# Two three-pass MLPs with rounded halves become one program of sixteen groups with plain fp32 products

## What is computed

```python
    xt = x_text + y                      # y: convolution result, scaled and shifted
    h = layernorm(xt, g_ffn, b_ffn)
    h = gelu(h @ W1 + b1) @ W2 + b2      # 512 -> 2048 -> 512
    xt = xt + h
    return layernorm(xt, g_norm_out, b_norm_out)
x = _layernorm(x + xattn(x, ...))
# second MLP; the linear maps around its gelu are folded into w3, b3, w4 earlier in the kernel
x = _layernorm(x + (gelu(x @ w3 + b3) @ w4 + b_con + down_bias))
```

## Time and profile before

| what | value |
|---|---|
| median of three runs | 5240.5 us |
| profiled execution, its time | 5239.47 us |
| profiled execution, first to last instruction (span) | 5237.8 us |
| span of the two MLP stages, from the barrier ahead of m1 | 3601.8 to 5237.8 us |
| TensorE matmul busy, of the span | 4067.8 us (78%) |
| mean granted TensorE clock | 0.88 of full speed |

### The profile page before, as it was taken

One profiled execution on the slowest core, in us unless ns is written; L12 is line 12 of the kernel. 1 busy time (PEld: TensorE's weight loads), 2 busy tenths in 40 slices (PEclk: granted clock), 3 DMA queues, 4 the chain that ended last, 5 costly groups with the idle time before them and its releaser, 6 DMA issues. The chain is left out here.

```text
span 5237.8 us, 64936 instructions
## 1 busy us (share of the span) xinstructions
PE 4067.8 (78%) x20932; PEld 3324.4 (63%) x20932; DVE 2781.6 (53%) x9228; ACT 1439.7 (27%) x2178; POOL 1430.1 (27%) x1238
## 2 busy tenths in 40 slices
PE   2243599975787784867769959696999996799998
PEld 2241277763676774756748847575788885688887
DVE  8965334443898998998815545423243433222222
ACT  1125423323555553545510010122111110211111
POOL 2530000000212111112106603202576763233332
PEclk9556799987888887888889979897999998899999
DMA  0003412225010010010014322334121211200000
GB/s 11 18 20 101 125 55 79 81 66 183 27 43 29 10 40 27 18 33 29 7 68 143 136 93 108 126 111 136 58 77 60 72 62 46 69 23 26 18 28 18
DMA packets 236653, 325.12 MB, mean 62 GB/s; under 512 B 67154, under 2 KB 117202, under 8 KB 234066
## 3 DMA queue, kind: packets, MB, share of 16 engines
q1 hardware_dynamic: 144260, 170.98, 11.0%
q10 hardware_dynamic: 89568, 142.64, 8.0%
q0 software_dynamic: 2560, 8.39, 0.4%
HBM read 214.93 MB, written 107.00 MB: 61 GB/s over the span
## 5 line engine op out<-in xcount | busy, mean ns | idle before, releaser
L1459 PE MATMUL xa_ps_t<-xa_diag,xa_s_buf 128*128 128x128 f32 x4096 | 501.1, 283 | 166.8 <-DVE xa_s_buf L1640 99.1
L2785 DVE CAST m_act_hl<-m_g 128x512 fp32r<-128x512 f32 x256 | 138.0, 539 | 891.8 <-ACT m_g L2673 891.8
L1459 PEld LDWEIGHTS xa_ps_t<-xa_diag,xa_s_buf 128*128 128x128 f32 x4096 | 485.2, 197 | 196.8 <-DVE xa_s_buf L1640 116.2
L1588 DVE MAX8 xa_cand<-xa_s_buf 128x8 f32<-128x64 f32 x4096 | 535.0, 217 | 119.2 <-issue 56.9
L2534 POOL TENSOR_TENSOR m_act_hl<-m_g,m_act_hl 128x512 fp32r<-128x512 f32 x256 | 352.5, 1377 | 701.2 <-DVE m_act_hl L2785 701.2
L2673 ACT ACTIVATE m_g<-m_ps_h,m_b 128x512 f32<-128x512 f32 x256 | 176.5, 690 | 1103.9 <-PE m_ps_h L82 1103.9
L1404 POOL TENSOR_TENSOR xa_aT<-xa_a,xa_aT 128x512 fp32r<-128x512 f32 x128 | 159.8, 1270 | 1004.1 <-ACT xa_a L1524 1004.1
L80 PE MATMUL m_ps_h<-m_hT,m_w 128*128 128x512 f32 x1024 | 412.8, 403 | 12.3 <-DVE m_w L2764 7.6
L81 PE MATMUL m_ps_h<-m_hT,m_w 128*128 128x512 f32 x1024 | 405.0, 395 | 0.0
L82 PE MATMUL m_ps_h<-m_hT,m_w 128*128 128x512 f32 x1024 | 404.8, 395 | 0.0
L82 PE MATMUL m_ps_o<-m_w,m_act_hl 128*128 128x512 f32 x1024 | 404.4, 395 | 0.0
(11 more groups left out here) (371 smaller groups left out, 8411.5 us busy)
## 6 DMA issues: line engine op xcount, KB each, us to landing
at_xk<-in_x_dram SPq DMA_DIRECT2D x128, 128.0 KB, 2.7
spectrum<-df_yo ACTq DMA_DIRECT2D x32, 512.0 KB, 2.8
id_raw<-spectrum SPq DMA_DIRECT2D x32, 512.0 KB, 3.8
m_xt<-x ACTq DMA_DIRECT2D x64, 256.0 KB, 3.6
ky_raw<-in_ctx_dram SPq DMA_DIRECT2D x16, 768.0 KB, 6.4
xa_ks<-kt SPq DMA_DIRECT2D x48, 256.0 KB
xa_raw<-in_ctx_dram SPq DMA_DIRECT2D x32, 384.0 KB, 3.5
w<-bf_out_t SPq DMA_DIRECT2D x32, 256.0 KB, 2.4
```

Source lines behind the costliest of these rows:

```text
L1459: last = pe.matmul(ps_t[:, c // 4, c % 4, :], s_buf[:, t % 2, h, k0:k0 + P], diag[:, h, :], start=(h == 0 and c % 4 == 0), stop=(h == HEAD ...
L1588: dve.max(out=ranks[h][:, :, g], in_=s_buf[:, t % 2, h, g * SEG:(g + 1) * SEG])
```

## The change

One `stage_mlps` takes the place of the two calls. It has 16 groups, of which `mlp(g)` = 0 for the first eight and 1 for the rest, all written out in order without a loop. `mm3` is replaced by one `pe.matmul` on fp32 tiles; w1 and w2 have both MLPs' weights side by side where the two halves were. The halves' instructions are gone on all engines. The weights come by DMA straight into place: W1 and W2 in four slabs each at the start, w3 and w4 in one DMA of 4 MB each, issued while groups 2 and 3 run. g_ffn and b_ffn are now applied where ScalarE writes hT (`written`, four activations of 128x128 a tile). The three operations of `outer_sum`, on GpSimd before, are on VectorE (`outer`) for every tile. All loads and stores go through SyncE's queue in one order. The second MLP turns tiles straight from xt, which has three group slots. turn comes at chunks 4, 7, 10 and 13.

```diff
-        w1 = sb("w1", [P, 2, DC, HID], F32R)
-        w2 = sb("w2", [P, 2, HC, D], F32R)
...
-        xt = sb("xt", [P, 2, Q, D])
-        h = sb("h", [P, D])
-        hT = sb("hT", [P, 2, 2, DC, N], F32R)
-        act_hl = sb("act_hl", [P, 2, 2, N], F32R)
-        g32 = sb("g32", [P, N])
+        w1 = sb("w1", [P, 2, DC, HID])
+        w2 = sb("w2", [P, 2, HC, D])
...
+        xt = sb("xt", [P, 3, Q, D])
+        fac = sb("fac", [P, 2, 3, D])
+        h = sb("h", [P, 2, D])
+        hT = sb("hT", [P, 2, DC, N])
+        gelu = sb("gelu", [P, 2, N])
...
+                def load(g, q):
+                    i = Q * g + q
+                    if g >= 3:
+                        sp.wait_ge(s_n1, i - 3 * Q + 1)
+                    if mlp(g) == 0:
+                        if i >= 2:
+                            sp.wait_ge(s_mod, i - 1)
+                        for n, v in enumerate((conv, so_in, sh_in)):
+                            sp.dma_start(fac[:, q % 2, n, :], rows(v, i * P, P)).then_inc(s_in[q % 2], 16)
+                        src = rows(x1, i * P, P)
                     else:
-                        n = m - PIECES // 2
...
-                    sp.dma_start(xt[:, 1, m % Q, :], src).then_inc(s_raw[m % Q], 16)
+                        j = i - Q * HALF
+                        sp.wait_ge(s_tr, i - 1)
+                        sp.wait_ge(s_st[q % 2], 16 * (j // 2 + 1))
+                        src = rows(x2, j * P, P)
+                    sp.dma_start(xt[:, g % 3, q, :], src).then_inc(s_in[q % 2], 16)
...
+                load(0, 0)
+                load(0, 1)
+                up_slab(0)
+                load(0, 2)
+                down_slab(0)
+                load(0, 3)
+                for s in range(1, SLABS):
+                    up_slab(s)
+                    down_slab(s)
+                load(1, 0)
+                load(1, 1)
...
+                    outer = g >= 1 and mlp(g - 1) == 0
+                    if outer:
+                        again(g - 1, 0)
+                    if g + 1 < GROUPS:
+                        load(g + 1, 2)
+                    if outer:
...
+                    if g == 2:
+                        sp.dma_start(w1[:, 1, :, :], w3.rearrange("(c p) n -> p c n", p=P)).then_inc(s_v1, 16)
+                    if g == 3:
+                        sp.dma_start(w2[:, 1, :, :], w4.rearrange("(c p) n -> p c n", p=P)).then_inc(s_v2, 16)
...
+                for g in range(GROUPS):
+                    nxt = mlp(g + 1) if g + 1 < GROUPS else None
+                    if nxt == 0:
+                        modulate(g + 1, 0)
+                    for q in range(Q):
+                        if g >= 1:
+                            power("e", Q * (g - 1) + q)
+                        if nxt == 0:
+                            power("p", Q * (g + 1) + q)
+                            if q + 1 < Q:
+                                modulate(g + 1, q + 1)
+                        if g >= 1 and mlp(g - 1) == 0:
+                            power("f", Q * (g - 1) + q)
+                        if nxt is not None:
+                            bias(g + 1, q)
...
                     for c in range(DC):
-                        w_hi, w_lo = (w1[:, x, c, n * P:(n + 1) * P] for x in range(2))
-                        last = mm3(pe, ps_h[:, n % 2, :], w_hi, w_lo, hT[:, slot, 0, c, :], hT[:, slot, 1, c, :],
-                                   start=(c == 0), stop=(c == DC - 1))
+                        last = pe.matmul(ps_h[:, n % 2, :], w1[:, mlp(g), c, n * P:(n + 1) * P], hT[:, g % 2, c, :],
+                                         start=(c == 0), stop=(c == DC - 1))
...
-                        a_hi, a_lo = (act_hl[:, n % 2, x, q * P:(q + 1) * P] for x in range(2))
-                        last = mm3(pe, ps_o[:, q, :], a_hi, a_lo, w2[:, 0, n, :], w2[:, 1, n, :],
-                                   start=(n == 0), stop=(n == HC - 1))
+                        last = pe.matmul(ps_o[:, q, :], gelu[:, n % 2, q * P:(q + 1) * P], w2[:, mlp(g), n, :],
+                                         start=(n == 0), stop=(n == HC - 1))
...
-                if modulated:
-                    pe.wait_ge(s_c, 16 * 6)
-                    for m in range(PIECES // 2):
...
-                        pe.wait_ge(s_raw[m % Q], 16 * (m // Q + 1))
-                        for r in range(4):
-                            n = 4 * q + r
-                            last = pe.matmul(ps_o[:, 0, c * HC + n:c * HC + n + 1], xt[:, 1, m % Q, r * P:(r + 1) * P],
-                                             bf[:, c:c + 1], start=True, stop=True)
...
-                pe.wait_ge(s_wlo, PIECES)
-                up(0, 0, 0, True)
...
+                pe.wait_ge(s_const, 1)
+                for q in range(Q):
+                    turn(0, q)
+                up(0, 0)
+                for g in range(GROUPS):
                     for n in range(HC):
-                        if not last and n >= 5 and (n - 5) % 3 == 0:
-                            turn(g + 1, 1 - slot, (n - 5) // 3)
+                        if g + 1 < GROUPS and n >= 4 and (n - 4) % 3 == 0 and (n - 4) // 3 < Q:
+                            turn(g + 1, (n - 4) // 3)
                         if n < HC - 1:
-                            up(g, slot, n + 1, first)
-                        elif not last:
-                            up(g + 1, 1 - slot, 0, False)
-                        down(g, n, first)
-                in_groups(pe, group)
+                            up(g, n + 1)
+                        elif g + 1 < GROUPS:
+                            up(g + 1, 0)
+                        down(g, n)
...
+                def written(g, q):
+                    act.wait_ge(s_tr, Q * g + q + 1)
...
+                    to = hT[:, g % 2, :, q * P:(q + 1) * P]
+                    if mlp(g) == 0:
+                        for c in range(DC):
+                            last = act.activation(to[:, c, :], ps_t[:, q % 2, c * P:(c + 1) * P], ACT.Identity,
+                                                  scale=gf[:, c:c + 1], bias=bf[:, c:c + 1])
...
+                def outer(g, q):
+                    i = Q * g + q
+                    ek = e[:, q % 2, :]
+                    dve.drain()
+                    dve.tensor_tensor(ek, ek, g_row[:, :], ALU.mult)
+                    dve.drain()
+                    dve.tensor_tensor(ek, ek, b_row[:, :], ALU.add)
+                    dve.drain()
+                    dve.wait_ge(s_xr, 16 * (i + 1))
+                    dve.tensor_tensor(ek, ek, xr[:, :], ALU.add).then_inc(s_e, 1)
...
+                for g in range(GROUPS):
+                    nxt = mlp(g + 1) if g + 1 < GROUPS else None
+                    if g >= 1:
+                        for q in range(Q):
+                            add(g - 1, q)
...
+                    for q in range(Q):
+                        if g >= 1:
+                            variance("e", xt[:, (g - 1) % 3, q, :])
+                        if nxt == 0:
+                            var_p(g + 1, q)
+                        if g >= 1:
+                            norm_e(g - 1, q)
+                            if mlp(g - 1) == 0:
+                                outer(g - 1, q)
+                        if nxt == 0:
+                            norm_p(g + 1, q)
+                        if g >= 1 and mlp(g - 1) == 0:
+                            var_f(g - 1, q)
+                            norm_f(g - 1, q)
+                for q in range(Q):
+                    add(GROUPS - 1, q)
+                    dve.drain()
+                    variance("e", xt[:, (GROUPS - 1) % 3, q, :])
+                    norm_e(GROUPS - 1, q)
```

More of the change, by code:

```diff
@@ L2470, in again @@
                     sp.wait_ge(s_e, i)
[L2471 to L2482 removed]
+                    sp.dma_start(xr[:, :], rows(x1, i * P, P)).then_inc(s_xr, 16)
@@ L2484, in _ @@
+                for q in range(Q):
+                    store(GROUPS - 1, q)
+                for k in range(2):
+                    sp.wait_ge(s_st[k], 16 * Q * GROUPS // 2)
             @block.gpsimd
@@ L2551, in _, with modulate @@
-                in_groups(pool, group)
+                def modulate(g, q):
+                    pool.wait_ge(s_in[q % 2], loaded(g, q))
+                    y, so, sh = (fac[:, q % 2, n, :] for n in range(3))
+                    pool.tensor_tensor(y, y, so, ALU.mult)
+                    pool.drain()
+                    pool.tensor_tensor(y, y, sh, ALU.add)
+                    pool.drain()
+                    pool.tensor_tensor(xt[:, g % 3, q, :], xt[:, g % 3, q, :], y, ALU.add).then_inc(s_mod, 1)
@@ L2681, in group @@
[L2681 to L2690 removed]
+                        if g or n >= 2:
+                            act.wait_ge(s_m2, HC * g + n - 1)
```

435 lines of the change are left out of this document (142 added, 293 removed).

## The result

The changed kernel takes **5447.7 us** (median of four runs, 5447.1 to 5452.3), the kernel before 5238.0 us (median of four, 5232.4 to 5240.9). The ratio is 1.0404, 95% interval 1.0386 to 1.0422: 4% slower. The forecast was 5445 us, in a range of 5425 to 5480.

The account below looks back on a forecast made before the run. The prediction took TensorE's matmuls, 99.7% busy in the groups, to bound the kernel. Its terms, +330 - 81.8 - 41.8 - 0.5 = +206 on 5239.5 us, gave 5445 us, range 5425 to 5480.

Parts of the forecast that it names:

- Price of the product: In both MLPs' groups, a plain fp32 product takes 0.8587 us against 0.6975 for three fp32r records: +330 us over 2048 products.
- The second start: Between the two MLPs, barrier, rounding and new first tile vanish and the second weights' loads are hidden: -81.8 us.
- The first start: Before the first MLP's first product, 72.8 us led by rounding becomes 31 us led by GpSimd: -41.8 us.
- The chain: At the first start, first tile's landing, four GpSimd modulations, then norm, turn and hT activations: 31 us in sum.
- Moved work: Inside the groups, work moved to VectorE, ScalarE and SyncE's queue stays hidden under TensorE's products and costs nothing.
- 15 us of slack: At a group's begin, the next h is ready after 2.8 + 9 us, its first turn due at 27.5 us.
- Tail: After the last product, add, variance and norm follow each other by tile: 15.3 instead of 15.8 us, -0.5 us.
- Sum: Whole kernel: 330 - 81.8 - 41.8 - 0.5 = +206 us on the profiled execution's 5239.5 us.
- rival 1: In the products, a plain record costs what an fp32r record does, 0.465 us a product: 4639 us in all; chance 4%.
- Rival 2: In the products, plain records pay for traffic as fp32r does, 5.4 ns each, +22 us: 5467 us; chance 17%.
- Rival 3: At the next group's first turn, h comes late and TensorE waits; 10 us in seven groups is 5515 us; chance 7%.

Follow-up runs that it names:

- the first experiment: The kernel before with its two stages kept, each of the 2048 products one plain fp32 product instead of three rounded ones: 5568.3 us, ratio 1.0635.

## Why the prediction was right

By its own terms:

- **Price of the product.** 2048 x (0.8587 - 0.6975) = +330 forecast. The groups went from 1465.6 to 1792.5 us, +326.9; with the edit alone in two stages the time went from 5238 to 5568. Two windows of plain fp32 in other stages, 246 records together, were enough to price 4096 of them. The group's other 2.3 us became 2.1 (111.99 - 128 x 0.8587).
- **The second start.** -81.8 forecast; it is gone, and the second weights are hidden: uncovered they cost 13.4 us by the medians and 15.1 by the groups, where the estimate was 22 at most.
- **The first start.** -41.8 forecast, -34.5 measured (72.8 to 38.3). This term was mis-sized. The chain was the right one, and laid bare it takes 31.0 us, but I priced each tile's load as if it had the queues to itself once its factors were free. Loads of the third and fourth tile landed 7.6 and 10.4 us after their issue, the rows of before gave 3.6. They shared the 16 DMA engines with the slabs and with the small loads: the window's DMA share is 1.03, and the loads came down to 5.7 and 7.3 us when the small loads were issued later, and to 4.1 and 4.2 with the slabs behind the tiles too. GpSimd's holes make 6 of the 7.3 us. Most of the rest lies behind the last modulation, 7.2 us to the first product instead of 5.4: the norm took 1.40 us instead of 0.55 beside GpSimd, and the hT writes 1.5 instead of 1.1.
- **Moved work.** Zero forecast, zero measured, but not by the numbers given. I had VectorE's three operations of `outer` at 0.69 us each. Two of the three, and the norm behind them, take 1.60 and 1.48 when GpSimd works beside them:

```profile
3876.36 0.69 DVE L2718 TENSOR_TENSOR m_e<-m_e,m_g_row 128x512 f32<-128x512 f32 x1
3876.64 1.53 POOL L2540 TENSOR_TENSOR m_fac<-m_fac 128x512 f32<-128x512 f32 x1
3877.12 1.60 DVE L2720 TENSOR_TENSOR m_e<-m_e,m_b_row 128x512 f32<-128x512 f32 x1
3878.32 1.53 POOL L2542 TENSOR_TENSOR m_fac<-m_fac 128x512 f32<-128x512 f32 x1
3878.80 1.60 DVE L2723 TENSOR_TENSOR m_e<-m_e,m_xr 128x512 f32<-128x512 f32 x1
3879.99 1.53 POOL L2544 TENSOR_TENSOR m_xt<-m_xt,m_fac 128x512 f32<-128x512 f32 x1
3880.32 1.48 DVE L2698 TENSOR_SCALAR m_h<-m_xt,m_mv_p,m_rstd_p 128x512 f32<-128x512 f32 x1
...
3900.35 0.60 PE L2596 MATMUL m_ps_t<-m_ident,m_h 128*128 128x128 f32 x4
```

The last row is TensorE's: `h` is written at 3881.8 and its turn starts at 3900.35, 18.5 us later, where the forecast had 15 us of slack. From the first addition (3870.14) to `h` it is 11.7 us, 11.8 forecast; the slack is larger since the additions begin 2.5 us before the group's last product ends.

- **Tail.** 15.3 forecast, 15.2 measured.
- **Sum.** +206 forecast, +210.0 measured between the two profiled executions' last stretches. The terms' errors are -3 in the products and +7.3 in the start, and they offset each other in part. The total came out nearer than its worst term, and that is in part luck: the profiled execution took 5452.3 us, 7 above the forecast, and the median of the four lies 4.6 under it. The range's lower end of 5425 is 5 us lower than its own terms make it (5445 - 9 - 6 = 5430).

The rivals: rival 1 falls by 0.429 a record over 1792 us and by 5568 us in the first experiment. The Trainium skill has true fp32 go through the array in four passes (FP8 and Floating Point Precision, TensorE Precision Notes). A product's 0.858 us would then be four of 0.2147, but the trace shows two records and not how many passes a record holds. Counted so, plain fp32 ran under 0.227 a pass already in the earlier trace rows; the prediction's "no stream of it goes under 0.227" holds for fp32r alone. The Trainium skill gives 131 ns as sustained for a matmul of 512 columns (TensorE: Matmul & The Clock Gate, Back-to-back issue gap). No stream of fp32 or fp32r here comes near that. Rival 2 falls too: a group takes 111.99 us under a mean of 63 GB/s in the first MLP and under 18 in the second. Its premise was weak already in the earlier trace rows: the rounded groups took 732.5 us at 61 GB/s, with GpSimd busy for 481 us, and 733.1 at 20 GB/s with 223, so what separates 0.2271 in one stage from 0.2325 in another is hardly that. Rival 3 falls by the 18.5 us between `h` and its turn and by groups without a wait; its sign, TensorE waiting for m_h, is there only in the start.

## What to carry to other kernels

Before replacing several rounded products by one plain one, count passes by the step between records in a stream (0.2325 us a rounded pass, 0.858 us a plain product of the same size): on an engine that is 99.7% busy at full clock, three rounded passes are cheaper than one plain product, however much work the plain one takes off the other engines. Where a change has two parts, run each alone; here one was worth -124 us and was buried under the other's +330. And in a start where everything loads at once, order the loads by who waits for them, and keep slow ones out of a queue whose engine has work to do.

## What was not expected of the hardware

- A load that writes 4-byte pieces down a column is small and slow, and the load issued right behind it is held in its issue. The two up biases, 8 KB each, landed 12.2 and 12.1 us after their issue. Behind the first, the second one's issue took 3.9 us, and behind that the next load's 6.7 on ScalarE (3606.20 and 3610.15 above); on SyncE the second's took 8.2. On GpSimd's queue the two took 1.2 us each, but neither had a column load right before it, so nothing shows that this queue is better. By the Trainium skill (DMA: Bandwidth & Descriptors, Rules for kernel authors), an access whose last dimension isn't contiguous becomes one descriptor per element. The start agrees: from 3604 to 3640 us, 5599 of 11121 packets are under 512 bytes, and the four column loads have 5120 elements. These rows add that it keeps the issuing engine from its compute for that long. Column loads are not the only ones: SyncE's 1 MB slabs in the same start, behind others of their kind, took up to 4.2 us to issue. What the two have in common was not tried.
- VectorE's 128x512 operations on SBUF go from 0.69 to 1.60 us and from 0.55 to 1.48 beside GpSimd's, and once to 4.99 beside four of GpSimd's instructions in a row, by the rows above. It cost nothing in the groups because 18.5 us lay between `h` and its turn; in a start, where the norm is on the path, it costs.
- Plain fp32 is 0.2147 us a pass, if it is four, and fp32r 0.2325 in the same place: the plain stream would then be 8% quicker a pass. Why the rounded one runs slower here than in the stage ahead (0.2271) was not tried.
